# Four layers of cross attention on one core: products over the whole stage, both halves of the keys on GpSimd, and a shorter first unit

## The reference

```
layer 0: xn = rmsnorm(x); K, V from rmsnorm(ctx) (1444 keys); x1 = xn + softmax(Q K / sqrt 8) V Wo + bo
layer 1: Q from x1, K, V from ctx (1444 keys), mask; x2 = layernorm(x1 + softmax(Q K) V Wo + bo)
layer 2: Q from x2, K, V from the first 100 rows of ctx, causal; a = layernorm(x2 + softmax(Q K) V)
         x3 = a + W2 gelu(W1 a + b1) + b2
layer 3: Q from x3, K, V from ctx (1444 keys); out = layernorm(x3 + softmax(Q K) V)
```

## Time and profile before

| | |
|---|---|
| median of three runs (lowest, highest) | 1085.7 us (1081.01, 1086.39) |
| the profiled execution: its own time, its span | 1088.03 us, 1086.2 us |
| PE busy, PEld busy | 945.0 us (87%), 555.8 us (51%) |
| DVE, ACT, POOL busy | 856.5 us (79%), 733.3 us (68%), 369.8 us (34%) |
| mean granted PE clock | 0.969 of full speed |
| chain that ended last, by engine | PE 57%, DVE 24%, ACT 7%, issue 6%, POOL 4% |

### The profile page before, as it was taken

One profiled execution on the slowest core, in us unless ns is written; L12 is line 12 of the kernel. 1 busy time (PEld: TensorE's weight loads), 2 busy tenths in 40 slices (PEclk: granted clock), 3 DMA queues, 4 the chain that ended last, 5 costly groups with the idle time before them and its releaser, 6 DMA issues.

```text
span 1086.2 us, 43882 instructions
## 1 busy us (share of the span) xinstructions
PE 945.0 (87%) x18826; PEld 555.8 (51%) x18826; DVE 856.5 (79%) x1800; ACT 733.3 (68%) x1644; POOL 369.8 (34%) x387
## 2 busy tenths in 40 slices
PE   0679989999989999999989898988888898989996
PEld 0235555555555555555555454555545454555653
DVE  4787887887877898889886877878787978779852
ACT  1146767767767787778766676767667676777776
POOL 5854344434323113311351515252524243321100
PEclk9787999999999999999998999999999999999999
DMA  8232213213212323332231212121212122021200
GB/s 211 76 83 85 61 53 85 77 51 84 71 50 84 101 64 90 91 101 55 81 96 31 88 42 71 32 71 32 77 35 77 37 68 77 27 84 50 55 5 6
DMA packets 63641, 73.74 MB, mean 68 GB/s; under 512 B 8131, under 2 KB 59115, under 8 KB 63319
## 3 DMA queue, kind: packets, MB, share of 16 engines
q1 hardware_dynamic: 63446, 70.92, 23.2%
HBM read 50.35 MB, written 18.15 MB: 63 GB/s over the span
## 4 chain that ended last, share of the span: by engine, by line
PE 57%; DVE 24%; ACT 7%; issue 6%; POOL 4%; SPq 1%; DMA 1%; POOLq 0%; ACTq 0%; DVEq 0%
PE ring L592 21%; PE acc L760 13%; PE sexp L592 12%; DVE mx L1159 9%; PE ring L635 5%; DVE mneg L1165 4%; DVE mx L1157 3%; ACT probs L1015 2%; POOL kbd L510 2%; PE ring L817 1%; PE ring L612 1%; DVE kp L1136 1%; SPq L471 1%; PE ring L771 1%; DVE ssq L1121 1%
## 5 line engine op out<-in xcount | busy, mean ns | idle before, releaser
L1159 DVE TENSOR_TENSOR mx<-ring,mx 120x400 f16<-120x400 f32 (+1 forms) x1056 | 560.2, 565 | 142.9 <-PE ring L592 138.6
L1015 ACT ACTIVATE probs<-sexp 120x400 f32<-120x400 f32 (+1 forms) x1152 | 533.7, 511 | 169.0 <-PE sexp L592 164.7
L592 PE MATMUL ring<-qx,krep 96*32 96x400 f16 (+2 forms) x4608 | 411.0, 346 | 38.8 <-DVE mx L1159 15.6
L592 PE MATMUL sexp<-qx,krep 97*32 97x400 f16 (+2 forms) x4608 | 407.4, 340 | 10.1 <-ACT probs L1015 6.2
L760 PE MATMUL acc<-probs,vx 120*18 120x200 f32 (+1 forms) x4608 | 254.3, 337 | 0.9 <-ACT probs L1015 0.7
L592 PEld LDWEIGHTS ring<-qx,krep 96*32 96x32 f16 (+2 forms) x4608 | 131.0, 98 | 127.6 <-DVE mx L1159 38.2
L592 PEld LDWEIGHTS sexp<-qx,krep 97*32 97x32 f16 (+2 forms) x4608 | 130.7, 96 | 103.8 <-ACT probs L1015 37.8
L527 POOL TENSOR_TENSOR qx<-qs,headmask 96x400 f16<-96x400 f16 x96 | 79.7, 860 | 262.6 <-DVE qs L1146 262.6
L760 PEld LDWEIGHTS acc<-probs,vx 120*18 120x18 f32 (+1 forms) x4608 | 131.0, 99 | 69.2 <-issue 5.0
L494 POOL TENSOR_TENSOR ct<-ctf,ct 128x480 f16<-128x480 f32 (+1 forms) x72 | 80.9, 1123 | 5.8
L635 PE MATMUL ring<-wv,ct 128*120 128x128 f16 (+1 forms) x864 | 64.1, 224 | 14.4 <-ACT vx L978 11.6
(11 more groups left out here) (133 smaller groups left out, 889.2 us busy)
## 6 DMA issues: line engine op xcount, KB each, us to landing
krep<-kept SPq DMA_DIRECT2D x144, 120.0 KB, 2.6
ctf<-in_ctxT SPq DMA_DIRECT2D x16, 722.0 KB
kept<-kp SPq DMA_DIRECT2D x48, 240.0 KB, 2.9
krep<-kept SPq DMA_DIRECT2D x72, 121.0 KB, 2.9
kept<-kp SPq DMA_DIRECT2D x24, 242.0 KB, 2.8
nat<-in_ctx SPq DMA_DIRECT2D x8, 720.0 KB
maskexp<-maskmax SPq DMA_DIRECT2D x8, 281.2 KB, 3.5
anymask<-in_mask SPq DMA_DIRECT2D x1, 1128.1 KB, 7.0
```

The source lines that it names most:

```text
L592: last = run(out[g:g + m], w[:, g:g + m], x, **flags)
L1015: act.activation(probs[0:r, j % PR, :], sexp[j % SR][0:r, 0:QW], ACT.Exp).then_inc(sem["probs_ready"], 1)
L1159: op = dve.tensor_tensor(dst, src, dst, ALU.max)
```

## The change

1. The tables `AT`, `AT2` and `AT2_FF` place the side products differently: the keys at steps 10, 22 and 30 instead of 9, 12 and 15, the values at 24, 27 and 33, layer 2's scores at 23 to 28, its scale at 12, its Gelu at 19. DVE's `power` comes at steps 25 and 28 instead of 29 and 32.
2. ACT reads the keys once from the bank into a new f32 tile `kf`, and the bank is free then. POOL makes both f16 parts from `kf`. DVE's part of this is gone. POOL's order gets `keys(prep, 0)` between the contexts and `spread2`, `keys(prep, 1)` behind `spread`, and `keys(prep, 2)` at the end.
3. The mask's bytes are cast by POOL instead of ACT, behind the roots.
4. SP loads the next transposed context before it keeps the keys, and replicates the first third of the keys before it keeps the other two; the second third is replicated after the third one is kept.
5. The first unit: constants are waited for in four portions, the first unit's context is split by ACT and DVE straight from the bank, DVE squares the first span itself, x and weights are prepared at steps of the first stages, seven small preparations move to stage 1, and ACT does one exp at its start.

The core of the diff:

```diff
-AT = {"ct0": 0, "ct1": 3, "ct2": 6, "O": 7, "k0": 9, "k1": 12, "OT": 13, "k2": 15, "wo": 16, "xT": 17, "q": 19,
-      "v0": 22, "v1": 24, "v2": 26, "mk0": 28, "mk1": 30, "mk2": 32, "scale": 30, "mt0": 36, "mt1": 37, "mn": 41}
-
-AT2 = {"cx": 4, "kqv": 7, "s0": 17, "s1": 19, "s2": 21, "s3": 23, "e0": 27, "e1": 28, "e2": 29, "e3": 30,
-       "pt0": 31, "pt1": 33, "pt2": 34, "pt3": 35, "a": 42, "o": 44, "out": 45}
-AT2_FF = {"out": 0, "scale": 13, "at": 18, "h": 23, "w2": 29}
+AT = {"ct0": 0, "ct1": 3, "ct2": 6, "O": 7, "k0": 10, "OT": 12, "wo": 15, "xT": 18, "q": 20, "k1": 22, "v0": 24,
+      "mk0": 25, "v1": 27, "mk1": 28, "k2": 30, "mk2": 31, "v2": 33, "power": 25, "scale": 32, "mt0": 36, "mt1": 37, "mn": 41}
+
+AT2 = {"cx": 2, "kqv": 5, "s0": 23, "s1": 25, "s2": 26, "s3": 28, "e0": 29, "e1": 31, "e2": 32, "e3": 34,
+       "pt0": 32, "pt1": 34, "pt2": 35, "pt3": 38, "a": 42, "o": 44, "out": 45}
+AT2_FF = {"out": 0, "scale": 12, "at": 16, "h": 19, "w2": 27}
...
-            READ[f"k{g}"] = ("k_lo", g + 1)
+            READ[f"k{g}"] = ("k_read", g + 1)
...
-                if s.prep is not None:
-                    for g in range(3):
-                        keep_keys(s.prep, g)
-                    replicate(s.prep, 0, s.exp, NSTEP // 3)
                 if s.load is not None and s.load.L:
                     load_transposed(s.load, s.prep)
+                if s.prep is not None:
+                    keep_keys(s.prep, 0)
+                    replicate(s.prep, 0, s.exp, NSTEP // 3)
+                    keep_keys(s.prep, 1)
+                    keep_keys(s.prep, 2)
+                    replicate(s.prep, 1, s.exp, 2 * NSTEP // 3)
                 if s.post is not None and s.post.L == 3:
                     store(s.post)
-                if s.prep is not None:
-                    replicate(s.prep, 1, s.exp, 2 * NSTEP // 3)
                 if s.top is not None:
                     maximum_row(s.top)
...
+                for name, dst, src in (("ident_in", ident[:, :], ident_in[0]), ("ident_in", cols[:, :], cols_in),
+                                       ("wk_in", wk[:, :, :], w_qkv[:, :, T * PARTS:T * PARTS + D].rearrange("l c n -> c l n")),
+                                       ("x_in", xall[:, :, :], x_in.rearrange("b s d -> s b d")),
+                                       ("x_in", wq[:, :, :, :], w_qkv[:, :, 0:T * PARTS].rearrange("l c (t p) -> c l t p", t=T)),
...
+            def keys(u, g):
+
+                _, c0, n, _ = groups()[g]
+                pool.wait_ge(*at("k_read", u, g + 1))
+                if g == 0:
+                    for i in range(3):
+                        pool.wait_ge(*at(f"k_kept{i}", u, 0))
+                pool.tensor_copy(kp[:, 0, c0:c0 + n], kf[:, c0:c0 + n]).then_inc(sem["k_high"], 1)
+                pool.wait_ge(*at("k_high", u, g + 1))
+                pool.tensor_tensor(kp[:, 1, c0:c0 + n], kf[:, c0:c0 + n], kp[:, 0, c0:c0 + n], ALU.subtract
+                                   ).then_inc(sem["k_lo"], 1)
...
+            def mask_bytes(u):
+
+                pool.wait_ge(*at("mask_loaded", u, 16))
+                for g in range(3):
+                    _, c0, n, _ = groups()[g]
+                    pool.tensor_copy(maskb[:, c0:c0 + n], mask8[:, c0:c0 + n]).then_inc(sem["mask_copied"], 1)
...
-                for c0, c1, r in SPANS:
+                for c0, c1, r in SPANS[1:] if u is UNITS[0] else SPANS:
...
             def stage(s, n):
-                if s.prep is not None:
+                if s.prep is not None and s.prep is not UNITS[0]:
                     for g in range(3):
                         context(s.prep, g, s.exp)
+                if s.prep is not None:
+                    keys(s.prep, 0)
                 if s.att2 is not None:
                     spread2(s.att2)
                 if s.ff2 is not None:
                     root(s.ff2)
                 if s.post is not None and s.post.L == 3:
                     root(s.post)
+                if s.prep is not None and s.prep.L == 1:
+                    mask_bytes(s.prep)
                 if s.load is not None and s.load.L == 0:
                     squares(s.load)
                 if s.prep is not None:
                     spread(s.prep, s.post)
+                    keys(s.prep, 1)
                 if s.post is not None and s.post.L == 1:
                     root(s.post)
                 if s.load is not None and s.load.L == 0:
...
                 if s.att2 is not None:
                     for t in range(T):
                         less_maximum(s.att2, t)
+                if s.prep is not None:
+                    keys(s.prep, 2)
 
             pool.memset(half[:, :], -0.5).then_inc(sem["pool_ready"], 1)
             pipeline(UNITS, stage, last=-3)
+            pool.wait_ge(sem["x_power"], 1)
+            pool.tensor_tensor(rinvx[:, :], ssqx[:, :], half[0:S, 0:B], ALU.pow).then_inc(sem["x_root"], 1)
+            pipeline(UNITS, stage, first=-2, last=-2)
             for i in range(2):
                 pool.memset(vx[:, i, :, :], 0.0).then_inc(sem["pool_ready"], 1)
                 pool.wait_ge(sem["pool_ready"], 2 + 2 * i)
...
             pool.memset(v2[:, :, DH:DH + 1], 1.0).then_inc(sem["pool_ready"], 1)
-
-            pool.wait_ge(sem["x_power"], 1)
-            pool.tensor_tensor(rinvx[:, :], ssqx[:, :], half[0:S, 0:B], ALU.pow).then_inc(sem["x_root"], 1)
-            pipeline(UNITS, stage, first=-2)
+            pipeline(UNITS, stage, first=-1)
 
...
                     act.wait_ge(*at("ct_low", before, 3))
+                if u is UNITS[0]:
+                    act.mul(ct[:, 0, 0, c0:c0 + n], bank(f"ct{g}", u)[:, 0:n], cols[:, COLC["gkv"]:COLC["gkv"] + 1]
+                            ).then_inc(sem["ct_high"], 1)
+                    return
...
             def keys(u, g):
 
                 _, c0, n, _ = groups()[g]
-                if g == 0:
-                    for i in range(3):
-                        act.wait_ge(*at(f"k_kept{i}", u, 0))
+                act.wait_ge(*at("k_lo", u, g - 2))
                 act.wait_ge(*at("k_filled", u, g + 1))
-                dst, src = kp[:, 0, c0:c0 + n], bank(f"k{g}", u)[:, 0:n]
+                dst, src = kf[:, c0:c0 + n], bank(f"k{g}", u)[:, 0:n]
                 bk = COLC[f"bk{u.L}"] if u.L else 0
                 op = act.activation(dst, src, ACT.Identity, bias=cols[:, bk:bk + 1]) if u.L else act.copy(dst, src)
-                op.then_inc(sem["k_high"], 1)
+                op.then_inc(sem["k_read"], 1)
 
...
                         queries(s.prep)
-                    for g in range(3):
-                        if s.prep is not None and s.prep.L == 1 and j == AT[f"mk{g}"] - 4:
-                            mask_bytes(s.prep, g)
...
-            act.wait_ge(sem["const_in"], 16 * 15)
+            act.wait_ge(sem["pool_ready"], 1)
+            act.activation(warm[:, :], half[:, 0:1], ACT.Exp)
+            act.wait_ge(sem["ident_in"], 32)
...
+            def context(u, g):
+
+                _, c0, n, _ = groups()[g]
+                dve.wait_ge(*at("ct_high", u, g + 1))
+                dve.scalar_tensor_tensor(out=ct[:, 0, 1, c0:c0 + n], in0=bank(f"ct{g}", u)[:, 0:n],
+                                         scalar=cols[:, COLC["gkv"]:COLC["gkv"] + 1], in1=ct[:, 0, 0, c0:c0 + n],
+                                         op0=ALU.mult, op1=ALU.subtract).then_inc(sem["ct_low"], 1)
+
+            def split(w, high, low):
+                step(dve.tensor_copy(high, w))
+                return dve.tensor_tensor(low, w, high, ALU.subtract)
+
+            def keys_weights():
+
+                dve.wait_ge(sem["wk_in"], 16)
+                split(wk[:, :, :], wk16[:, 0], wk16[:, 1]).then_inc(sem["wk_ready"], 1)
+
+            def input_power():
+
+                dve.wait_ge(sem["x_in"], 64)
+                sqx = kbd2[0:S, :, :, :].rearrange("s a h k -> s (a h k)").bitcast(F32)[:, 0:B * D].rearrange("s (b d) -> s b d", d=D)
+                step(dve.tensor_tensor(sqx, xall[:, :, :], xall[:, :, :], ALU.mult))
+                step(dve.tensor_reduce(ssqx[:, :], sqx, AX, ALU.add))
+                dve.tensor_scalar(ssqx[:, :], ssqx[:, :], 1.0 / D, EPS[0], ALU.mult, ALU.add).then_inc(sem["x_power"], 1)
+
+            def input_scaled():
+
+                dve.tensor_copy(headmask16[:, :], headmask[:, 0:HT])
+                dve.tensor_scalar(wq[:, :, :, :], wq[:, :, :, :], SCALE, None, ALU.mult).then_inc(sem["wq_ready"], 1)
+                dve.tensor_copy(ident16[:, :], ident[:, :])
+                dve.wait_ge(sem["x_root"], 1)
+                step(dve.tensor_tensor(xall[:, :, :], xall[:, :, :], rinvx[:, :].unsqueeze(2).broadcast_to([S, B, D]), ALU.mult))
+                dve.tensor_tensor(xall[:, :, :], xall[:, :, :],
+                                  rows[:, ROW["gq"], :].unsqueeze(1).broadcast_to([S, B, D]), ALU.mult
+                                  ).then_inc(sem["x_ready"], 1)
+
+            def values_weights():
+
```

(81 more changed lines are left out.)

66 lines of the change are left out of this document (17 added, 49 removed).

## The result

The changed kernel takes 1101.65 us (median of four runs, 1101.06 to 1102.81) against 1085.55 before; the ratio is 1.0158, with a 95% interval of 1.0129 to 1.0188. Forecast were 1064 us and a gain. The span of the profiled execution is 1100.0 us, 13.8 more than before.

A forecast was written before the change was run, and what follows sets the result against it. No engine was full to the end; PE's chain plus stalls set the stages. Terms -18 - 16 + 25 - 4 - 3 - 6 = -22 us from 1088.0 gave 1066, as median 1064 us; range 1022 to 1088.

The forecast's parts named there:

- 36.3 from 714.9: Stages 13 to 19: time from the root's arrival at 714.9 to the stage's end, 36.3 us, making the stage 54.2 us.
- the gain that was to outweigh them: All stages outside 13 to 19 together: 47 us won, against 25 us lost in those seven.
- Rival 1: Stages 13 to 19: the root's wait costs all it can, +8 us a stage, kernel 1095 us; chance 0.17.
- point of decision: Stages 13 to 19: rival 1 decides from a loss of 47 / 7 = 6.7 us a stage on.
- The path to the release: Stages 13 to 19: from step 7's output transposes at 702.1 through first keys and kbd to the root at 714.9.
- Gelu: Stages 13 to 19, behind the root's wait: Gelu with two table loads of 1.28 us, about 3 us lost.
- The clock: Stages 13 to 19: PE falls to half pace, 1.2 instead of 2.4 GHz, after its gap; 2 us counted.
- SP at nothing: Late replica of the keys' second third, about step 38: costs nothing, hidden by 13 steps or some 9 us before use.
- Layer 1: Stages 6 to 11: PE floor about 32.5 us, 4.4 us of stalls, 2.6 won a stage, -16 us in all.
- Stage 12: Has kbd but no root to wait for; its 52.8 us should shrink by 4.
- The start: First unit: less waiting and fewer squares against a late second third of the keys; gain 2 to 12 us, 6 taken.
- The shared port: POOL and DVE: added POOL instructions can block two-input DVE operations; zero net, 0 to +1 us a stage.

The follow-up runs named there:

- e1: The changed kernel with POOL taking the root of ff2 ahead of keys(prep, 0) and spread2: 1043.93 us, ratio 0.9625.
- e2: The changed kernel with Gelu at step 23 and the product after it at step 29: 1087.57 us, ratio 1.0024 to the kernel before.
- e3: The changed kernel with POOL making the third group of keys ahead of normalise in layer-0 units: 1096.90 us, ratio 1.0103 to the kernel before.
- e9: The kernel before with one move, POOL taking the root of ff2 ahead of spread2: 1081.62 us, ratio 0.9977.
- e10: e8 with layer 3's four layer-norm parts of post at steps 21 to 24, its root behind the second keys: 1014.54 us, ratio 0.9357.
- e7: The changed kernel with POOL's order root of ff2, spread2, keys(prep, 0), so kbd comes ahead of the first keys: 1065.69 us, ratio 0.9834.
- e5: The kernel before with the change's step tables, power at steps 25 and 28, and SP's new order; keys and masks as before: 1060.20 us, ratio 0.9777.
- the fourth move: The edit e10 adds to the three moves of e8, layer 3's layer norm of post moved to steps 21 to 24: 1014.54 us.
- e8: The changed kernel with root of ff2 first, Gelu at step 23 and third keys ahead of normalise in layer-0 units: 1030.94 us, ratio 0.9498.

## Why the prediction was wrong

**The step that failed.** The mechanism against the change was the right one, in the right place: DVE waits at step 12 of stages 13 to 19 for a root that stands behind the first keys and kbd. e1 shows it by removing it. What failed first is the term behind the wait, "36.3 from 714.9": from DVE's release at 751.73 to the start of the next stage it measured 39.9 us. So these stages lost 6.0 us each and not 3.5. What failed next is the gain that was to outweigh them: 47 us in all other stages, of which 28.0 came.

| part | forecast | measured |
|---|---|---|
| start and stage 0 | -9 | -5.5 |
| stages 1 to 5 | -15 | -4.6 |
| stages 6 to 11 | -16 | -12.2 |
| stage 12 | -4 | -9.0 |
| stages 13 to 19 | +25 | +41.8 |
| stages 20 to 23 | -3 | +3.3 |
| sum | -22 | +13.8 |

Rival 1 had the right form. Its point of decision, 6.7 us a stage, rests on the 47; with 28.0 it is 4.0, and the stages lost 6.0.

**The path to the release** was right to 0.1 us (12.9 against 12.8).

**Gelu** was sized at 3 us lost. It stands at step 19, and the queries, which DVE needs at step 20, are behind its two table loads in ACT's queue. So not only ACT was late but DVE a second time, and PE stood again; between 757.3 and 763.7 PE has 2.3 us without any matmul. Putting Gelu back gains 1.8 us a stage in e2, and takes stage 20, which the forecast had among the gains, from 45.0 to 41.7. The root's move alone takes it to 41.6 (e1). The forecast had read Gelu's price off the chain of before, where the queries stood four steps ahead of it: what is queued behind the moved step was not looked at there.

**The clock** was sized at 2 us, for one fall. In the stage shown there were two, 3.9 us at 0.50 and 2.8 us at 0.54 of full speed in the windows above; about half of that, 3.3 us, is an estimate of the cost. The second fall came in three of the seven stages. In stages 17 to 19, where the clock was 1.00 before, all of it is new.

**SP at nothing** was wrong in layer 0. The distance that was to hide it was measured to the second replica's use, and that was right but for the start. Behind that replica stood the row of maxima, with no distance at all. The layer-0 stages won 0.9 instead of 3.0. e3 shows 0.6 of it. For the rest, the chain of e3 has DVE's reductions at the end of the stage, which the text had named and not priced; no run took them away.

**Layer 1** was near: 2.0 won, 2.6 forecast. PE was taken to have 32.5 us of work; at 34.06 busy of 34.50 it is nearly full, so that floor was some 1.5 us low.

**Stage 12** won 9.0 and not 4. Of this, 4.0 is the clock of the one execution of before that was profiled (e9 has 48.8 there); the remaining 5 are near the forecast.

**The start** with stage 0 won 5.5, where 6 + 3 were forecast; executions of the same program differ by 2.8 us in this stretch, so most of the miss may be that. The replica's wait came where it had been put.

```profile
17.15 2.64 PE L646 MATMUL ring<-ident,nat 121*128 121x121 f32 x12 [17.15 <-POOL nat L574]
...
33.00 1.19 PE L626 MATMUL ring<-qx,krep 96*32 96x400 f16 x12 [2.86 <-POOL qx L547]
...
47.26 0.53 PE L626 MATMUL ring<-qx,krep 96*32 96x400 f16 x4 [4.63 <-DMA krep<-kept]
```

PE's first work in the **timeline of the kernel after** is at 17.15, on the normalised context, not at 21.00 on a constant; the first maxima are at 33.00; and the tile of step 3 waits 4.63 us for `krep`.

**The shared port** was costed at zero net. In the changed kernel this held, for a reason that does it no credit: DVE stood idle beside kbd, waiting for the root. With that wait gone it was the next thing: about 5 us a stage go with it in stages 17 to 19 (e10, with the thinner pile), and about 5 in 13 to 16 when kbd comes 4 us earlier (e7). By the Trainium skill ("SBUF — State Buffer", "SBUF: two separate sides"), the blocked side stands until the holder's instruction ends; the trace agrees, with ends within 0.2 us of each other in e7.

**Still open.** Why e3's layer-0 stages are not below 37.5 was read from the chain and not tried. What e5 leaves between the two ways of making the keys was not split into DVE's and ACT's part. What sets the clock in a given execution is open too: the same stands of PE went with either level in stage 12 (e9).

## What to carry to other kernels

When work is put into an in-order queue, list what stands behind it in that queue and who waits for that, also in the DMA queue: the work itself may be free and the 0.55 us instruction behind it cost 58 us. Price a stall by what follows it too: in e10's place 2 us on DVE went with 5 us a stage, through the clock and through the next step that was late, while two holds of 1.6 and 1.5 us in e1 left the clock at 1.00 and the stages at 46.9 us. And before a difference between stages of two profiles is put down to an edit, compare the granted clock in them: here it moved a stage by 4 us where nothing had been changed. When one move is undone to test it, look at which waits the move had been hiding; the best version here came from the fourth move.

## What the hardware showed that was not expected

The lower clock came with stands of PE of a few microseconds: in all seven stages while PE stood for the root (0.50 over 3.9 us of work in stage 16), in three of them again after the queries' wait (0.54 over 2.8 us), and in e8 after PE had stood 2.4 us. In e10, where PE's longest stand in stage 18 is 0.9 us, it did not come. But the length of one stand does not tell it: in stage 12 PE stands for 1.7 us at most in the kernel before and in e9, and the one has 0.50 for some 10 us, the other never.

Beside a product on POOL of 1600 elements, a DVE operation of 128 elements took up to 2.52 us in place of 0.28, when both of its inputs were in SBUF; DVE's operations with an input in a bank went on beside it at their usual 0.57.
